# First block of a three-block kernel: first norm's rows on ScalarE with a shift from GpSimd, its statistics behind the third lookup unit, rows of x loaded behind the gate and up indices

## The reference, cut to what matters

```
x = hidden                                   # 1 x 2048 tokens x 256 channels, fp32
x = x + 0.5 * ffn(layernorm(x))              # first block, the "front"
x = x + mamba(layernorm(x))                  # in-projection, conv, scan, gate, out-projection
x = x + 0.5 * ffn(layernorm(x))              # same weights as the first

def layernorm(x): return (x - mean(x)) / sqrt(var(x) + 1e-5)
def ffn(x):                                  # weights are looked up in a table of 16 values
    gate = x @ lut[gate_idx].T               # 256 -> 688
    up   = x @ lut[up_idx].T                 # 256 -> 688
    return (silu(gate) * up) @ lut[down_idx].T   # 688 -> 256
```

## Time and profile before

| | value |
|---|---|
| three runs, us | 518.34, 519.86, 520.81 |
| the profiled execution's own time / its span, us | 518.19 / 516.5 |
| mean granted TensorE clock | 0.980 of full speed |
| TensorE matmul busy | 473.5 us, 92% of the span |
| VectorE busy | 374.7 us, 73% |
| ScalarE busy | 284.0 us, 55% |
| GpSimd busy | 160.9 us, 31% |
| index units on TensorE | first lookup at 7.63 us, fourth unit done at 36.27 us |

### The profile page before, as it was taken

One profiled execution on the slowest core, in us unless ns is written; L12 is line 12 of the kernel. 1 busy time (PEld: TensorE's weight loads), 2 busy tenths in 40 slices (PEclk: granted clock), 3 DMA queues, 4 the chain that ended last, 5 costly groups with the idle time before them and its releaser, 6 DMA issues.

```text
span 516.5 us, 17146 instructions
## 1 busy us (share of the span) xinstructions
PE 473.5 (92%) x7486; PEld 396.9 (77%) x7486; DVE 374.7 (73%) x742; ACT 284.0 (55%) x513; POOL 160.9 (31%) x216
## 2 busy tenths in 40 slices
PE   4899999999989995986899999999978999999997
PEld 3557797988878884875688878887867778898987
DVE  7998936466769999844788888788859866556543
ACT  3658535253328999798556665567635423323241
POOL 1100040203042111114667676676746411000000
PEclk9999999999989999797999999999989999999999
DMA  8960080000000000100000000000350000101001
GB/s 206 207 241 1 1 339 7 0 3 1 0 1 0 3 0 0 42 22 3 4 6 4 5 4 6 4 5 4 134 220 4 4 2 0 42 7 35 22 21 42
DMA packets 7387, 21.31 MB, mean 41 GB/s; under 512 B 784, under 2 KB 5392, under 8 KB 6672
## 3 DMA queue, kind: packets, MB, share of 16 engines
q1 hardware_dynamic: 6832, 18.05, 10.7%
q10 hardware_dynamic: 480, 2.16, 1.8%
HBM read 12.87 MB, written 6.55 MB: 38 GB/s over the span
## 4 chain that ended last, share of the span: by engine, by line
PE 32%; issue 9%; POOL 8%; ACT 4%; DVE 3%; POOLq 0%; DVEq 0%; ACTq 0%
POOL w L1264 6%; PE intra L898 4%; PE seg L876 2%; PE yo L1016 2%; POOL tmp L1281 1%; PE XB L987 1%; PE new L999 1%; PE XB L68 1%; PE BG L68 1%; PE yo L70 1%; PE yo L68 1%; PE yo L69 1%; PE new L68 1%; PE XB L950 1%; PE new L70 1%
## 5 line engine op out<-in xcount | busy, mean ns | idle before, releaser
L1264 POOL TENSOR_TENSOR w<-xdt,ends 32x512 f32<-32x512 f32 (+3 forms) x63 | 66.5, 1074 | 4.2 <-PE prior L994 2.8
L657 DVE SCALAR_TENSOR_TENSOR cv<-pre,vec,cv 128x512 f32<-128x512 f32 x72 | 52.9, 750 | 5.5 <-ACT cv L695 3.8
L1043 ACT ACTIVATE seg<-seg 128x512 f32<-128x512 f32 x64 | 35.8, 578 | 32.6 <-PE seg L876 32.5
L1131 DVE TENSOR_TENSOR mmat<-seg,gs 128x512 f32<-128x512 f32 x64 | 42.5, 684 | 11.3 <-ACT seg L1043 11.3
L528 POOL TENSOR_TENSOR n_rstd<-n_ve,m_half 128x4 f32<-128x4 f32 x12 | 13.1, 1088 | 120.2 <-DVE n_ve L523 120.1
L876 PEld LDWEIGHTS seg<-abk,m_seg 96*32 96x32 bf16 x2048 | 20.7, 97 | 24.1 <-DVE mmat L1131 12.7
L68 PE MATMUL pj<-n_xT,win 128*128 128x512 f32 x88 | 35.6, 405 | 2.3 <-PEq L130 2.3
L1056 ACT ACTIVATE f_hT<-f_h 128x512 fp32r<-128x512 f32 (+1 forms) x24 | 15.2, 632 | 40.1 <-DVE f_h L1142 40.1
L69 PE MATMUL pj<-n_xT,win 128*128 128x512 f32 x88 | 35.0, 397 | 0.0
L876 PE MATMUL seg<-abk,m_seg 96*32 96x64 bf16 x2048 | 27.2, 196 | 8.4 <-ACT ends L1047 4.7
L70 PE MATMUL pj<-n_xT,win 128*128 128x512 f32 x88 | 34.8, 395 | 0.0
(11 more groups left out here) (264 smaller groups left out, 1454.9 us busy)
## 6 DMA issues: line engine op xcount, KB each, us to landing
wgu_dram<-wgu SPq DMA_DIRECT2D x1, 2816.0 KB, 8.2
wgu<-wgu_dram SPq DMA_DIRECT2D x1, 2816.0 KB, 10.5
out<-x_res SPq DMA_DIRECT2D x8, 256.0 KB, 2.1
x_res<-in_x SPq DMA_DIRECT2D x1, 1536.0 KB, 23.6
wd_dram<-wd SPq DMA_DIRECT2D x1, 1536.0 KB, 11.6
wd<-wd_dram SPq DMA_DIRECT2D x1, 1536.0 KB, 13.8
win_raw<-in_in_w SPq DMA_DIRECT2D x1, 1408.0 KB, 26.4
gu_idx<-in_gu ACTq DMA_DIRECT2D x3, 352.0 KB, 9.1
```

Of the source, the lines that this page charges most:

```text
L657: dve.scalar_tensor_tensor(dst, pre[:, x, k:k + GN].rearrange("p (t c) -> p t c", c=P), cw[:, x, k:k + 1], dst, ALU.mult, ALU.add).then_in ...
L1043: act.activation(seg[u_ % 2][:, :, :], seg[u_ % 2][:, :, :], ACT.Exp).then_inc(s["exp_ok"], 1)
L1131: dve.tensor_tensor(mmat[a % 2][:, i, :], seg[u_ % 2][:, :, :], gs[a % 2][:, i].unsqueeze(2).broadcast_to([P, IU, HEADS]), ALU.mult).then_ ...
L1264: pool.tensor_tensor(heads(w[r, n, :]), heads(xdt[a % 2][r, :]), ends[a % 2][r, n * HEADS:(n + 1) * HEADS].unsqueeze(2) .broadcast_to([Q * ...
```

## The change

- The split of unit 0 goes: `FIRST`, the semaphores `gu_first` and `mask_first`, the two DMAs of 512 columns and the loop at L280. Each index unit is one DMA on each queue, and a mask of unit 0 is made whole.
- On SyncE's queue the first 512 tokens of x are loaded behind all four index units.
- On VectorE `dve_stats(0)` stands behind the masks of unit 2 (before: unit 1), and `dve_xn(0)` is gone.
- On GpSimd `pool_shift(0)` follows `pool_rstd(0)`: it makes -mean * rstd in two instructions of 128 x 4.
- On ScalarE `act_xn(0)` makes the four tiles of xn as Identity(rstd * x + shift), behind `evac(2)` and ahead of `act_hi(0)`.
- `Norm` has one more tile, `shift` (128 x 4), and two semaphores. TensorE's order is the same.
- `masks` gets arguments `first` and `end` that no call sets.

```diff
--- before.py
+++ after.py
@@ -54,7 +54,7 @@
 PAIRS = LUT // 2
 HG = 16
 EPS = 1e-5
-NORM_WORDS = GT * 6 + GROUPS * GT * (2 + 1 + 1) + GT * HID + 2 * KC * 2 * GN
+NORM_WORDS = GT + GT * 6 + GROUPS * GT * (2 + 1 + 1) + GT * HID + 2 * KC * 2 * GN
 MUP_Z, MUP_X = 0.25, 0.5
 
 GUC = 11
@@ -138,7 +138,6 @@
         win_raw, wout_raw = sb("win_raw", [P, KC, PCH * P]), sb("wout_raw", [P, 4, HID])
         GU_D, GU_A, DN_D, DN_A = 6, 2, 5, 2
         W = GUC * P
-        FIRST = 4
         with ExitStack() as first:
             big = lambda n: first.enter_context(nc.sbuf_tensor(n, [P, W], F32R))
             mask_d, mask_a = [big(f"mask_d{n}") for n in range(GU_D)], [big(f"mask_a{n}") for n in range(GU_A)]
@@ -153,7 +152,6 @@
         bank = ((gate[0][:, :], gate[1][:, :], up[0][:, :]), (up[1][:, :], flat(down[0]), flat(down[1])))
         vec_in, x0_in, x_in, win_in, wout_in, *gu_in = map(sem, (
             "vec_in", "x0_in", "x_in", "win_in", "wout_in", "gu_in0", "gu_in1", "gu_in2", "gu_in3"))
-        gu_first, mask_first = map(sem, ("gu_first", "mask_first"))
         dn_in, ident_ok, half_ok, entry_ok, zeroed, hz, two_ok, lut_ok, table_ok = map(sem, (
             "dn_in", "ident_ok", "half_ok", "entry_ok", "zeroed", "hz", "two_ok", "lut_ok", "table_ok"))
         mask_ok, amask_ok, used_ok, aused_ok, evac_ok, split_hi, wout_s = map(sem, (
@@ -181,12 +179,10 @@
         @block.sync
         def _(sp):
             sp.dma_start(T["vec"][:, :], A["vec"]).then_inc(vec_in, 16)
-            sp.dma_start(gu_idx[0:H64, 0, 0:GN], A["gu"][:, 0, 0:GN]).then_inc(gu_first, 16)
-            sp.dma_start(gu_idx[0:H64, 0, GN:], A["gu"][:, 0, GN:]).then_inc(gu_in[0], 16)
-            sp.dma_start(gu_idx[0:H64, 1, :], A["gu"][:, 1, :]).then_inc(gu_in[1], 16)
+            sp.dma_start(gu_idx[0:H64, 0, :], A["gu"][:, 0, :]).then_inc(gu_in[0], 16)
+            for q in range(1, QTR):
+                sp.dma_start(gu_idx[0:H64, q, :], A["gu"][:, q, :]).then_inc(gu_in[q], 16)
             sp.dma_start(T["x_res"][:, 0:GT, :], x_in_dram[:, 0:GT, :]).then_inc(x0_in, 16)
-            for q in range(2, QTR):
-                sp.dma_start(gu_idx[0:H64, q, :], A["gu"][:, q, :]).then_inc(gu_in[q], 16)
             sp.dma_start(dn_idx[0:H64, 0:HALVES, :], A["dn"]).then_inc(dn_in, 16)
             sp.dma_start(T["x_res"][:, GT:, :], x_in_dram[:, GT:, :]).then_inc(x_in, 16)
             sp.dma_start(win_raw[:, :, :], A["in_w"].rearrange("(k p) n -> p k n", p=P)).then_inc(win_in, 16)
@@ -221,6 +217,7 @@
             pool.memset(T["m_half"][:, :], -0.5).then_inc(half_ok, 1)
             pool.wait_ge(half_ok, 1)
             norm.pool_rstd(pool, 0)
+            norm.pool_shift(pool, 0)
             pool.wait_ge(aused_ok, QTR)
             pool.memset(hT[:, 0, FCH - 1, :].bitcast(F32), 0.0).then_inc(hz, 1)
             norm.pool_rstd(pool, 1)
@@ -244,8 +241,8 @@
 
         @block.vector
         def _(dve):
-            def masks(unit):
-                for p in range(1, PAIRS):
+            def masks(unit, first=1, end=PAIRS):
+                for p in range(first, end):
                     n = unit * (PAIRS - 1) + p - 1
                     if unit < QTR:
                         if n >= GU_D:
@@ -257,8 +254,6 @@
                         halves = 2 if d < FCH - 1 else 1
                         dst = low_d[m % DN_D][:, 0:HID * halves]
                         src = dn_idx[:, 2 * d:2 * d + halves, :].rearrange("p a c -> p (a c)")
-                    if unit == 0 and p < FIRST:
-                        dst, src = dst[:, GN:], src[:, GN:]
                     dve.tensor_scalar(dst, src, entry[:, p:p + 1], None, ALU.is_equal).then_inc(mask_ok, 1)
 
             lut = T["lut_pair"]
@@ -276,18 +271,13 @@
                                   ).then_inc(table_ok, 1)
             dve.wait_ge(entry_ok, 2 * PAIRS + 4)
             norm.dve_start(dve)
-            dve.wait_ge(gu_first, 32)
-            for p in range(1, FIRST):
-                dve.tensor_scalar(mask_d[p - 1][:, 0:GN], gu_idx[:, 0, 0:GN], entry[:, p:p + 1], None, ALU.is_equal
-                                  ).then_inc(mask_first, 1)
-            for unit in range(QTR):
+            for unit in range(QTR - 1):
                 dve.wait_ge(gu_in[unit], 32)
                 masks(unit)
-                if unit == 1:
-                    dve.wait_ge(x0_in, 16)
-                    norm.dve_stats(dve, 0)
-                if unit == 2:
-                    norm.dve_xn(dve, 0)
+            dve.wait_ge(x0_in, 16)
+            norm.dve_stats(dve, 0)
+            dve.wait_ge(gu_in[QTR - 1], 32)
+            masks(QTR - 1)
             norm.dve_lo(dve, 0)
             dve.wait_ge(dn_in, 32)
             dve.wait_ge(aused_ok, QTR)
@@ -327,9 +317,7 @@
 
         @block.scalar
         def _(act):
-            act.dma_start(gu_idx[H64:P, 0, 0:GN], A["gu"][:, 0, 0:GN]).then_inc(gu_first, 16)
-            act.dma_start(gu_idx[H64:P, 0, GN:], A["gu"][:, 0, GN:]).then_inc(gu_in[0], 16)
-            for q in range(1, QTR):
+            for q in range(QTR):
                 act.dma_start(gu_idx[H64:P, q, :], A["gu"][:, q, :]).then_inc(gu_in[q], 16)
             act.dma_start(dn_idx[H64:P, 0:HALVES, :], A["dn"]).then_inc(dn_in, 16)
 
@@ -363,7 +351,6 @@
                 ins.then_inc(evac_ok, 1)
 
             act.wait_ge(entry_ok, 2 * PAIRS + 4)
-            act.wait_ge(gu_first, 32)
             for unit in range(2):
                 act.wait_ge(gu_in[unit], 32)
                 ramp_mask(unit)
@@ -373,6 +360,7 @@
                     act.wait_ge(gu_in[unit + 2], 32)
                     ramp_mask(unit + 2)
                 if unit == 2:
+                    norm.act_xn(act, 0)
                     norm.act_hi(act, 0)
             act.wait_ge(dn_in, 32)
             ramp_mask(QTR)
@@ -423,8 +411,6 @@
                 for p in (*range(1, PAIRS), 0)[first:last]:
                     if p:
                         n = unit * (PAIRS - 1) + p - 1
-                        if n < FIRST - 1:
-                            pe.wait_ge(mask_first, n + 1)
                         pe.wait_ge(mask_ok, n + 1)
                         mask = mask_d[n % GU_D] if unit < QTR else low_d[(n - QTR * (PAIRS - 1)) % DN_D]
                     else:
@@ -496,11 +482,13 @@
         self.rstd = sb("rstd", [P, GROUPS, GT])
         self.xn = sb("xn", [P, GT, HID])
         self.xT = sb("xT", [P, 2, KC, 2 * GN], F32R)
+        self.shift = sb("shift", [P, GT])
         self.base = 0
         self.pt = banks
         self.stat_ok, self.mv_ok, self.ve_ok, self.rstd_ok = map(sem, ("stat_ok", "mv_ok", "ve_ok", "rstd_ok"))
         self.xn_ok, self.pt_ok, self.hi_ok, self.lo_ok = map(sem, ("xn_ok", "pt_ok", "hi_ok", "lo_ok"))
         self.stat_seen = sem("stat_seen")
+        self.neg_ok, self.shift_ok = sem("neg_ok"), sem("shift_ok")
 
     def rows(self, g, t):
         return self.T["x_res"][:, (g % GROUPS) * GT + t, :]
@@ -527,6 +515,20 @@
         pool.wait_ge(self.ve_ok, g + self.base + 1)
         pool.tensor_tensor(self.rstd[:, g % GROUPS, :], self.ve[:, g % GROUPS, :], self.T["m_half"][:, 0:GT], ALU.pow
                            ).then_inc(self.rstd_ok, 1)
+
+    def pool_shift(self, pool, g):
+        pool.tensor_scalar(self.shift[:, :], self.mv[:, g % GROUPS, :, 0], -1.0, None, ALU.mult).then_inc(self.neg_ok, 1)
+        pool.wait_ge(self.neg_ok, 1)
+        pool.wait_ge(self.rstd_ok, g + self.base + 1)
+        pool.tensor_tensor(self.shift[:, :], self.shift[:, :], self.rstd[:, g % GROUPS, :], ALU.mult
+                           ).then_inc(self.shift_ok, 1)
+
+    def act_xn(self, act, g):
+        act.wait_ge(self.shift_ok, 1)
+        act.wait_ge(self.pt_ok, g + self.base + 1)
+        for t in range(GT):
+            act.activation(self.xn[:, t, :], self.rows(g, t), ACT.Identity, scale=self.rstd[:, g % GROUPS, t:t + 1],
+                           bias=self.shift[:, t:t + 1]).then_inc(self.xn_ok, 1)
 
     def dve_xn(self, dve, g):
         dve.wait_ge(self.rstd_ok, g + self.base + 1)
```

## The result

The changed kernel takes 524.15 us (median of 8 runs, 522.31 to 525.31); beside it the kernel before takes 519.09 (516.74 to 520.81). The ratio is 1.0092, 95% interval 1.0069 to 1.0116: **slower by 0.9%, about 5 us**. The forecast was 523.4, or +3.5 us over the 519.86 shown with the kernel before; against the 519.09 measured now that rise is 1.6 us short, while the absolute time is 0.75 us short.

A forecast was written before the change was run, and what follows sets the result against it. VectorE's masks and what stands between them were taken to bound the front, ending at the fourth evacuation. A 1.3 us longer wait plus 2.2 for the clock gave +3.5 on 519.86: 523.4 us, range 519.8 to 525.4.

The forecast's parts named there:

- Whole masks, x behind the indices, statistics at 24.8 us: VectorE's front: masks from 6.7 us, 21 without a break to 24.82; x in time, at 25.8 us at the latest.
- Shift: GpSimd after the power: two small instructions taking 0.55 us (bounds 0.2 to 1.6), shift ready at 29.35 us.
- xn on ScalarE: Behind evac(2), from 29.5 us: four activations taking 2.07 us (bounds 1.38 to 2.8), ending at 31.6.
- TensorE's queue: Unit 3's lookups queue behind xn's transposes: 5.1 us idle in place of 2.56, plus 1.3 us with the clock up.
- The clock: TensorE's clock likely halves in the 5.1 us gap, slowing transposes and unit 3's lookups: 2.2 us (1.75 to 2.7).
- The slow start: TensorE's first three lookups, 1.17 us each until 11.13 us, read as the lower clock level; 0.64 us each afterwards.
- The sum: 1.3 us for the wait plus 2.2 for the clock: +3.5 us, median 523.4 us.
- The clock stays up: Rival: TensorE's clock does not fall in the gap before unit 3; only +1.3 us, 521.2 us; chance 0.24.
- Not slower: Rival: short chain to xn, transposes starting before 30.3 us, fourth unit 0.7 us earlier; 519.2 us; chance 0.07.
- table load: Rival: Identity needs a table load of 1.28 us on ScalarE ahead of xn; 524.7 us; chance 0.03.
- The late shift: Rival, shared with late x: shift up to 0.9 us late, x 1.0, clock low; 525 us; chance 0.06.
- Passed on one for one: Whatever moves the start of the fourth evacuation on ScalarE, 36.31 us, moves everything behind it by the same amount.

The follow-up runs named there:

- e6: Kernel before with only the split of unit 0 removed (whole masks); front 36.04 us against 36.31, one run.
- e8: Kernel before with only the first x DMA moved behind the index units; front 36.54 us against 36.31, one run.
- e2: Changed kernel with VectorE waiting for the shift before it makes unit 3's masks; 522.23 us, ratio 1.0084 to the kernel before.
- e3: Changed kernel with the transposes between the sixth and seventh lookup of unit 3 on TensorE; 518.24 us, ratio 1.0002 to the kernel before.
- e1: Changed kernel with 26 dummy matmuls on TensorE while it waits for xn; 523.2 us, ratio 1.0096 to the kernel before.
- the repeats: Second runs of the changed kernel with 26 dummy matmuls and of the changed kernel unaltered; ratios 1.0099 and 1.0109 to the kernel before.
- e4: Changed kernel with xn made by VectorE again, behind three masks of unit 3, and no shift; 523.36 us, ratio 1.01 to the kernel before.
- e11: Changed kernel unaltered, run again; 524.38 us, ratio 1.0109 to the kernel before.
- e5: Kernel before with shift on GpSimd and xn on ScalarE ahead of evac(2), statistics still behind unit 1; 518.63 us, ratio 0.9988.
- the warm-up kernel: Changed kernel with 26 dummy matmuls on TensorE during the wait for xn, run twice; 523.2 and 523.59 us, ratios 1.0096 and 1.0099.

## Why the prediction was right, and where it was off

- **Whole masks, x behind the indices, statistics at 24.8 us: right.** Masks from 6.74 (forecast 6.7), bn_stats at 24.85 (24.82), and each edit alone moves the front by 0.3 us at most (e6, e8). x landed 15.8 us after its issue at 3.76, at 19.6 us, not near the 25.8 of the bound.
- **Shift: the term that was mis-sized.** Forecast 0.55 us for the two small instructions, bounds 0.2 to 1.6; measured 28.71 to 30.50, 1.8 us, over the upper bound. The rows that it was taken from the earlier trace rows come from stretches in which VectorE makes no masks. Beside masks they wait; alone, in e2, they take 0.23 and 0.20 us, within the bounds. The first power of the kernel before, 1.62 us beside masks against 1.01 us for the shortest of its twelve, already told this, and the prediction used it without asking why it was long. The Trainium skill, "SBUF — State Buffer", section "SBUF: two separate sides", says that VectorE in its two-port mode and GpSimd hold a shared pair of ports exclusively, each for a whole instruction. e2 agrees, with 0.96 us beside masks against 0.23 alone; in which mode the masks ran no trace here shows.
- **xn on ScalarE: right in length,** 2.07 us as worked out, but it was the shift and not evac(2) that released it, at 30.53 instead of 29.5. TensorE's gap was 6.12 instead of 5.1 us.
- **TensorE's queue: right.** Unit 3's masks lay ready; moving the transposes gives 6.1 us back (e3).
- **The clock: right that it falls, low in its price.** Forecast 2.2 us, with bounds of 1.75 to 2.7; measured 2.8 (41.59 against 38.81 in e1) and 2.4 (41.16 against 38.71 in the repeats). It stayed low 5.8 us after work resumed, just beyond the 3.5 to 5.6 foreseen, and 4.5, 5.4 and 4.9 us in e2, e4 and e11. The prediction priced the slow transposes with matmuls of another line (+1.0); they took 1.62 us (32.66 to 34.28), +0.8 over the 0.85 of before, and the slow lookups cost the other 2.0. The time from TensorE's last matmul to the fall was 5.1 us here, 4.2 in e11, 3.0 in e4 and 2.6 in e2, so the 4.8 us read at 205.5 was not a limit that 5.1 only just passed. The rule on idle gaps in "HAM oscillation — how this bites in real kernels" of "TensorE: Matmul & The Clock Gate" in the Trainium skill held in every run with a gap of over 4 us (4.38, 4.97, 6.11 and 6.12 us). In e5 and e8 the clock fell after waits of 1.9 and 3.15 us as well.
- **The slow start.** The prediction read the pace of the first three lookups, 1.17 us, as the lower clock. The profile's clock row has 1.00 there (7.60 to 10.60 us), so that level is inferred from the length of the matmuls and not shown by the granted clock.
- **The sum.** 1.3 + 1.1 for the shift + 2.8 for the clock = 5.2; the trace has 5.3. The forecast rise of 3.5 us was 1.6 short of the 5.1 measured, both terms erring the same way. That 523.4 came so near to 524.15 is partly luck: the median it started from, 519.86, was 0.8 us above the one measured beside the changed kernel.
- **The rivals.** "The clock stays up" argued from the 2.56 us gap that did nothing; e5 and e8 show the clock falling just behind a wait in that same place, so one execution was thin evidence. "Not slower" needed transposes at 30.3; they came at 32.66. No table load came with Identity. The late shift was a rival at 0.06 together with x; x was in time, the shift was not.
- **Passed on one for one? As far as the projection, yes; beyond it, not shown.** From the end of the front to the first projection matmul it is 114.1 to 114.7 us in all fourteen profiles. The front is 5.3 us longer and the medians 5.1 (changed) and 4.5 us (e11), which fits. But the warm-up kernel and e4, with fronts only 2.4 to 3.4 us longer, have medians 3.7 to 5.3 us above. So the agreement of 5.3 and 5.1 is no measure of what each part is worth in the total; of the kernels that keep the late statistics only e3, which takes unit 3 out of the wait for xn, brings it back. In the profiled execution the total is 6.7 us longer: 5.3 in the front, 2.9 in the scan, and some 1.5 gained back elsewhere, 0.8 of it in the projection stage.

## What to carry to other kernels

When a step is taken off a busy engine, ask first who is queued behind its result in program order: here xn off VectorE made the front 0.7 to 1.6 us shorter when it stayed early, and 5.3 us longer when its input came after the third unit and TensorE's next unit stood behind it. A wait of several us on TensorE can be paid twice, once as idle time (6.1 us here) and once as slow matmuls after it (2.4 to 2.8 us). Check the total as well as the stage: two kernels here (the warm-up kernel, run twice, and e4) had a front 1.9 to 2.9 us shorter than the changed one, with no clear gain in the total. Take the price of a small GpSimd instruction from a stretch where VectorE does what it will be doing beside it.

## What the runs showed of the hardware that was not expected

- GpSimd instructions of 128 x 4 take 0.96 and 0.75 us beside VectorE's 128 x 1408 masks and 0.23 and 0.20 us alone; the power takes 1.62 against 1.01.
- TensorE's clock fell to half in idle gaps of 4.4, 5.0 and 6.1 us, and shortly after gaps of 1.9 (e5) and 3.15 us (e8), but not around gaps of 1.2, 1.5, 1.6, 2.56 and 2.63 us in the same place. What decides it for a gap below 4 us is open.
- A 16-byte tile that nothing uses may lengthen a stage 200 us later (scan 175.0 against 170.8 us); likely, not proven. In the last block the tile, used or not, goes with 0.3 us less, in all fourteen profiles.
